# GpSimd starts scaling a finished weight half one DVE level later, in a quantised-weight FFN kernel

## The reference

```python
# _L0_cond: O = I = 2048, GROUP = 128
lora_delta = lora_B @ lora_A * (LORA_ALPHA / LORA_RANK)          # x 0.5
cb = codebook / clip(max(abs(codebook)), 1e-08)                  # 32 values
scale = exp(scale_log)                                           # one per 128 inputs
normalized = (weight + lora_delta).reshape(O, I // GROUP, GROUP) / scale
thresholds = (cb[:-1] + cb[1:]) * 0.5                            # 31
quantized = cb[searchsorted(thresholds, normalized, side='left')]
w_eff = (quantized * scale).reshape(O, I) + lora_delta           # by value
h = x @ w_eff.T
# _L0_ffn: 8 experts, rank 16
result = h @ W_base.T + b_base
ax, probs = h @ A_w.T, softmax(h @ router_w.T)
mixed = einsum('bseq,bse->bsq', einsum('bsr,erq->bseq', ax, cores), probs)
out = x + result + (mixed @ B_w.T) * 2.0
```

## Time and profile before

| | us |
|---|---|
| median of three runs | 2441.57 |
| profiled execution, its own time | 2441.73 |
| its span in the trace | 2439.9 |
| PE busy | 2328.5 (95%) |
| DVE busy | 1686.5 (69%) |
| ACT busy | 1414.2 (58%) |
| POOL busy | 1317.8 (54%) |

### The profile page before, as it was taken

The page is one execution under the profiler, slowest core; times in us unless marked ns, Lnnn a source line. Parts: engine busy times, 40 slices in busy tenths (PEclk is TensorE's granted clock), DMA queues, the critical chain, the costliest instruction groups (busy, mean ns, idle before and its releaser), DMA issues.

```text
span 2439.9 us, 30454 instructions
## 1 busy us (share of the span) xinstructions
PE 2328.5 (95%) x11648; PEld 2101.3 (86%) x11648; DVE 1686.5 (69%) x2007; ACT 1414.2 (58%) x1764; POOL 1317.8 (54%) x739
## 2 busy tenths in 40 slices
PE   3878889999999999999999999999999999999999
PEld 1444449999999989999999989999999988999998
DVE  7999997777777977888877967888863323333333
ACT  7999988788875666666646656666632321111111
POOL 5889887777893437777764436777750000110010
PEclk9998899999999999999999999999999999999999
DMA  5766773544334335676764435766754333555553
GB/s 194 244 245 227 257 263 139 182 166 159 144 132 134 118 98 184 223 240 217 241 220 141 118 96 186 239 218 231 234 203 119 100 98 140 193 195 189 186 193 148
DMA packets 121237, 442.58 MB, mean 181 GB/s; under 512 B 12754, under 2 KB 53074, under 8 KB 84178
## 3 DMA queue, kind: packets, MB, share of 16 engines
q1 hardware_dynamic: 121092, 440.64, 53.0%
HBM read 289.46 MB, written 151.13 MB: 181 GB/s over the span
## 4 chain that ended last, share of the span: by engine, by line
PE 82%; DVE 8%; ACT 4%; POOL 3%; DMA 1%; issue 1%; SPq 0%; DVEq 0%; POOLq 0%; ACTq 0%
PE m L652 20%; PE m L653 20%; PE m L654 19%; PE m L636 7%; PE m L638 7%; PE m L637 7%; DVE acc L940 5%; ACT mk L777 2%; PE m L609 1%; PE m L682 1%; POOL pp L1090 1%; ACT mp L783 1%; POOL tm L1086 1%; DVE kl L970 1%; POOL wr L1097 1%
## 5 line engine op out<-in xcount | busy, mean ns | idle before, releaser
L940 DVE SCALAR_TENSOR_TENSOR acc<-mk,dj,acc 128x1024 f32<-128x1024 uint8 x736 | 944.3, 1283 | 111.8 <-ACT mk L777 94.6
L652 PE MATMUL m<-gh,xh 128*128 128x384 f32 (+2 forms) x2560 | 904.6, 353 | 7.7 <-DVE gl L951 6.1
L653 PE MATMUL m<-gl,xh 128*128 128x384 f32 (+2 forms) x2560 | 899.4, 351 | 0.0
L654 PE MATMUL m<-gh,xl 128*128 128x384 f32 (+2 forms) x2560 | 896.8, 350 | 0.0
L777 ACT ACTIVATE mk<-wr,bj 128x1024 uint8<-128x1024 f32 x768 | 848.5, 1139 | 55.1 <-DVE acc L940 46.2
L652 PEld LDWEIGHTS m<-gh,xh 128*128 128x128 f32 x2560 | 482.4, 188 | 32.9 <-issue 6.4
L654 PEld LDWEIGHTS m<-gh,xl 128*128 128x128 f32 x2560 | 481.6, 188 | 23.7
L653 PEld LDWEIGHTS m<-gl,xh 128*128 128x128 f32 x2560 | 482.3, 188 | 21.6
L1107 POOL TENSOR_TENSOR xl<-xw,xh 128x512 fp32r<-128x512 f32 x128 | 174.9, 1367 | 562.0 <-ACT xh L819 562.0
L1090 POOL TENSOR_TENSOR pp<-pp,tm 128x1024 f32<-128x1024 f32 x192 | 465.2, 2423 | 16.0
L1086 POOL TENSOR_SCALAR tm<-mp,dj 128x1024 f32<-128x1024 uint8 x224 | 255.6, 1141 | 207.0 <-ACT mp L783 194.0
(11 more groups left out here) (98 smaller groups left out, 1529.2 us busy)
## 6 DMA issues: line engine op xcount, KB each, us to landing
part<-part SPq DMA_DIRECT2D x192, 1036.0 KB, 6.6
rows<-in_wb SPq DMA_DIRECT2D x64, 1036.0 KB, 4.8
xw<-in_x SPq DMA_DIRECT2D x128, 256.0 KB, 3.1
out<-part SPq DMA_DIRECT2D x32, 1024.0 KB, 4.2
kw<-in_wb SPq DMA_DIRECT2D x144, 192.0 KB, 2.4
wr<-in_w SPq DMA_DIRECT2D x32, 512.0 KB, 7.6
dl<-delta SPq DMA_DIRECT2D x30, 512.0 KB, 5.9
delta<-ds SPq DMA_DIRECT2D x24, 512.0 KB, 3.3
```

The costliest lines, as they stand in the source:

```text
L652: e.matmul(R.m[c][:, 0:w], xh, gh, start=k == 0, stop=False)
L653: e.matmul(R.m[c][:, 0:w], xh, gl, start=False, stop=False)
L654: done = e.matmul(R.m[c][:, 0:w], xl, gh, start=False, stop=stop and k == n - 1)
L940: e.scalar_tensor_tensor(R.acc, R.mk[k % NM], R.dj[:, j:j + 1], R.acc, ALU.mult, ALU.add).then_inc(S["ac"], 1)
```

## The change

There are five edits. (1) In `effective`, POOL's scaling of a finished half q (q below 8) no longer waits for `cl` alone but for `ac`, DVE's level 0 of half q+1. (2) POOL's first mask scaling of half q+1 is put ahead of that (`spare_scaled`), and only the addition stands behind it (`spare_added`). (3) POOL's two `lora_b` operations wait for DVE's level 0 of half 0. (4) `BOOK_LAG` goes from 4 to 2. (5) The `rows_out` of blocks 0 to 2 comes one level sooner (j = 3 for 4), and eight `wide` places come one level later.

```diff
-BOOK_LAG = 4
+BOOK_LAG = 2
...
-            if j == 4 and 3 <= q <= 2 * N0 and q % 2:
+            if j == 3 and 3 <= q <= 2 * N0 and q % 2:
                 yield ("rows_out", (q - 3) // 2)
...
-    late = [(0, j) for j in range(6, 22, 2)] + [(1, j) for j in range(4)] + [(2, j) for j in range(4)]
+    late = [(0, j) for j in range(6, 22, 2)] + [(1, j) for j in range(1, 5)] + [(2, j) for j in range(1, 5)]
...
-    def spare(q, i):
+    def spare_scaled(q, i):
         k = NP * q + i
-        w = R.wr[raw_of(q)]
         e.wait_ge(S["mp"], k + 1)
         if k == 0:
             e.wait_ge(S["bk"], BOOK_READY)
-            e.wait_ge(S["n"], 1)
         else:
             e.wait_ge(S["pp"], k)
         e.tensor_scalar(R.tm, R.mp[k % 2], R.dj[:, NV + i:NV + i + 1], 0.0, ALU.mult, ALU.add).then_inc(S["tm"], 1)
-        if i == 0 and q:
-            e.wait_ge(S["cl"], q)
+
+    def spare_added(q, i):
+        k = NP * q + i
+        if i == 0:
+            e.wait_ge(S["n"], q + 1)
+            if q:
+                e.wait_ge(S["cl"], q)
         e.wait_ge(S["tm"], k + 1)
-        e.tensor_tensor(R.pp, R.pp if i else w, R.tm, ALU.add).then_inc(S["pp"], 1)
+        e.tensor_tensor(R.pp, R.pp if i else R.wr[raw_of(q)], R.tm, ALU.add).then_inc(S["pp"], 1)
 
     def effective(q):
         w = R.wr[raw_of(q)]
-        e.wait_ge(S["cl"], q + 1)
+        if q < 2 * N0:
+            e.wait_ge(S["ac"], NV * (q + 1) + 1)
+        else:
+            e.wait_ge(S["cl"], q + 1)
...
     normalise(0)
+    e.wait_ge(S["ac"], 1)
     lora_b(0)
...
             if j in SPARE_AT:
-                spare(q, SPARE_AT.index(j))
+                i = SPARE_AT.index(j)
+                if i or not 0 < q <= 2 * N0:
+                    spare_scaled(q, i)
+                spare_added(q, i)
...
         elif what == "effect":
+            if at[0] < 2 * N0:
+                spare_scaled(at[0] + 1, 0)
             effective(*at)
```

## The result

The changed kernel takes 2428.48 us (median of six runs, 2425.24 to 2430.06), the kernel before 2441.38 (six runs, 2439.25 to 2443.29) beside it. The ratio is 0.9946, 95% interval 0.9934 to 0.9959: 12.9 us faster. The profiled execution took 2429.68 us with a span of 2427.9. Forecast were 2426.8 us and a range of 2424 to 2432.

What follows compares the result with a forecast made beforehand. PE was taken to set the end behind the startup, whose halves DVE and POOL pace, so startup savings count one for one. Start 4.5, halves 8.8 and clock 1.6 made 14.9 off 2441.73: 2426.8 us, range 2424 to 2432.

Steps and rivals of the forecast that it cites:

- The start: Half 0, edits 3 and 4: DVE's 16-wide table steps no longer run beside POOL's `lbl`; everything behind comes 4.5 us sooner.
- The boundary: Each half's end: DVE's level 0 takes 1.29 for 3.03, 1.74 saved; POOL's first sum at 5.76 for 6.52, 0.76 saved.
- The halves: Halves 1, 4, 6, 8, paced by POOL, save 3.0; 3, 5, 7, paced by DVE, 5.0; half 2 0.8; sum 8.8.
- I count 0.2 off: Half 7: two deltas and five moved-up copies ahead of the fifth mask lower the odd halves' saving from 5.2 to 5.0.
- Edit 5 otherwise costs nothing: Halves: ACT's earlier copies find PE done, later delta DMAs cause no wait, at worst 1 us in half 2.
- half 2 term: Half 2, held by ACT: the saving lies between 0 and level 0's 1.74; the middle, 0.8, was taken.
- The clock: First token products: PE idle ahead falls from 4.76 to 3.5 us, so some 12 slow matmuls run faster, 1.6 less.
- E: Startup's end: PE's `rows` becomes the end, so nothing gained at the halves; decides only if 4 us longer; 2428 to 2430; 3%.
- A: First token products: forecast without the clock gain, PE falls to the slow level because idle exceeds 3.6 us; 2428.4; 25%.
- B: New DVE or ACT collision: half 2's low part meets POOL's second sum, or late mask scaling meets level 0; 2 to 4 us; 15%.
- C: Halves: only POOL's loop counts, ACT's masks hold odd halves to 0.76 saved each, not 1.7; 2429.7 to 2431; 7%.
- D: Boundaries: level 0 is long for its own sake, stays 3.03, POOL's first sum one us later per half; 2445.0; 3%.

Runs made afterwards that it cites:

- the small instruction: Kernel before plus one 8-column one-input POOL tensor_scalar per half below 8, between the last sum and the scaling's wait; 2440.66 us, one time.
- small tensor_tensor: Kernel before plus one 8-column two-input POOL tensor_tensor per half below 8, between the last sum and the scaling's wait; 2443.1 us, one time.

## Why the prediction was right, and where its steps were not

**The bound.** Right: the gain in the startup is 12.30 us at the first token product, and the time fell by 12.9. From the first product to the end of the span the changed kernel took 2076.2 and 2074.8 us in two traces, the kernel before 2076.0; over all traces it lies between 2072.6 and 2078.8 with no order by the edits that I can see. The 1.7 us by which the first trace was longer than the kernel before behind its 13th product shrank to 0.3 in the second.

**The start.** 4.5 forecast, 4.67 measured, 4.58 in the kernel with that alone. Right with its mechanism, `lbl` on the way of DVE's table steps. POOL's slack in half 0 was there: its last sum ended at 55.31 and DVE wanted it at 57.42.

**The boundary.** The durations came as forecast: level 0 1.29, first sum at C + 5.71 (5.76), `wr<-wr,dl` 2.35. The cause was put in the wrong edit; the sum came out since the kernel has both. I gave the end of the collision to the wait for level 0. The runs show that the reordered mask scaling alone brings level 0 to 1.29, that the wait alone brings nothing (0.9997), and that the wait on top of the reorder costs 0.23 in each half that POOL paces.

**The halves.** Forecast 8.8, measured 7.64. Halves 1 to 6 and 8 came 7.2 to the forecast 7.3. The step that failed is half 7, "I count 0.2 off": it is 1.1 more, and with either half of edit 5 taken back it is gone. The copies were counted, but not that the delta ahead of them would wait 1.00 for PE, whose `rows` of half 5 had run 31.12 us, starting at the slow clock (28.09 in the kernel before). With the delta places back that `rows` took 29.79, and half 7 36.35; with `rows_out` back 29.54 and 36.20. What the place of the copies adds to the late PE is argued above and not shown by a run of its own.

**Edit 5.** "Edit 5 otherwise costs nothing" holds for the delta places, but they were worth far more than my half 2 term says. With edits 1 and 2 and without them half 2 grows to 40.8, 2.9 over the kernel before. The 0.8 forecast there (0.93 measured) was right by luck, the sum of a loss that I had not seen and an edit that avoids it.

**The clock.** 1.6 forecast, and the first 12 products took 2.17 us in place of 3.66: 1.5 gained. The reason given was wrong, so the number is luck, and the totals, which spread over more than that, can't confirm it. I had 3.5 us of idle time ahead of them; it is 1.30. PE's last `rows` itself started at the slow clock, after 4.59 us idle, took 30.23 in place of 28.09, and so ended close to half 8. What I took as a rival of its own (E) is half true: PE's `rows` has become nearly the end. My price for it, "only if `rows` took 4 us more", was wrong. With `rows_out` back a `rows` of 30.99, 2.9 more than before, did decide, with 1.26 us from its end to the first product; the changed kernel has 1.30 there, so it lies within 0.04 us of that.

**Rivals.** A: its time, 2428.4, is nearest to the median, but the clock did come back. Of the 1.7 us between forecast and median half 7 is 1.1, and the rest lies within the spread of the times. B: in part. The A factor's low part took 1.55 in one trace of the changed kernel and 0.69 in the other, and POOL's sum behind it 2.67 and 2.36. It waited for the one-input mask scaling and not for the second sum, as I had written; and the 0.78 that I called its time with POOL free held 0.23 of waiting, since POOL's first sum ended at 109.09. The first mask's scaling was never in level 0's way, since it ends 0.1 ahead of C as worked out. C is refuted by halves 3 and 5, which save 1.5 and 1.65. D is refuted by level 0.

The prediction quoted a rule of the Trainium skill ("SBUF — State Buffer", section "SBUF: two separate sides"): whichever instruction starts first holds the pair. On holding it to the end the traces agree (1.90 and 1.1 us waited), also for a one-input GpSimd instruction, of which the prediction had no row: the low part took 1.55 and 0.84 us where 1.01 and 0.31 of the mask scaling were left, 0.54 more each time. On who is first they don't in the kernel before: DVE's record starts 0.05 earlier and POOL's instruction is served. With `rows_out` back it is the other way round in half 2: the mask scaling starts 0.04 earlier (103.32), and DVE's low part is served at once (0.69). The measurement decides: starts within 0.05 us of each other in the trace do not tell the winner.

## What to carry to other kernels

Where two engines contend at a handover, read which of the two paces the loop before choosing the loser, and test an order change and a wait apart: here the order change won the 1.74 us and the wait cost 0.23 in each half that POOL paces. What it may buy is certainty, since what decides a tie is open (DVE won 16 of 16 behind the large mask scaling without the wait, but 6 of 8 behind the small instruction). When a stall is taken out of a tight chain, look at every instruction that stood in its shadow (deltas, copies, a two-input instruction next to POOL), since they come onto the path one by one. Where terms of 0.1 to 2 us are at stake, read the starts and ends in the trace; the total can't tell edits of 1 to 2 us apart.

## What the runs showed of the hardware that I had not expected

- In the kernels in which POOL's scaling waits for the end of the half alone, DVE's level 0 and POOL's scaling start within 0.05 us in that order. Behind a two-input POOL instruction POOL was served first at every boundary of halves 1 to 8 (kernel before and small tensor_tensor, 8 of 8 each), behind the mask scaling DVE (8 of 8 in each of two kernels), behind an 8-column tensor_scalar DVE in 6 of 8.
- A DVE instruction with two inputs in SBUF also waits for a one-input POOL instruction: the 64x512 low part takes 0.69 us alone, and 1.55 and 0.84 with 1.01 and 0.31 of a 128x1024 tensor_scalar left.
- A one-input DVE tensor_scalar of 31 columns took 2.27 us beside POOL's 128x1024 two-input instruction, 0.18 without it.
- PE fell to the granted clock 0.50 in `rows` after only 2.27 us without an instruction, where it had done six short matmuls in the 6 us before (window 246.4 to 248.4); after 1.30 us idle behind a full `rows` it stayed at 1.00. So idle time right ahead doesn't tell it alone, as I had taken it to.
